# Four layers in one kernel: the first half's row maxima taken in fp32 before the operands are split

## The chip, the cores and the metric

The kernel runs on one core of one Trainium2 chip. The metric is the device time of one execution in microseconds. Engines: TensorE (PE; PEld for its weight loads), VectorE (DVE), ScalarE (ACT), GpSimd (POOL) and SyncE (SP), which here only issues DMAs. They run side by side and wait for each other by semaphores that the kernel sets by hand.

## What is computed

The input x is (4, 32, 32, 32): 4 images b, 32 channels, 32 x 32 pixels. Four layers follow, each on the normalised sum so far and added to it:

```python
x = x + volterra(norm(x))        # layer 0: 3x3 taps and their pairwise products
x = x + conv3x3(norm(x))         # layer 1
x = x + attention(norm(x))       # layer 2
x = x + hartley(norm(x))         # layer 3: transform, mix of modes, transform back
```

In layer 2 the image is projected (W_in); a 3x3 convolution gives q (all 1024 pixels), and two without padding give k and v (900 keys), in 4 heads of 8 channels. Per image and head: softmax over the keys of q.k, times v. The other three query and token pairs of the reference have a zero hidden state, so that of them only the mean of the value convolution over the image is left; it enters the gates as a bias (the "box sums"). Gates, a cell and an output projection end the layer.

## The kernel before

**Stages.** Layer 0 up to about 44 us, layer 1 to about 63, the projections of layer 2 to about 93, its attention to about 290, layer 3 to the end.

**Attention.** Queries are handled in 8 halves (2 halves of the pixels x 4 images), each with 4 heads and 4 tiles of 128 queries. exp(q.k - max) needs each query's maximum over 900 keys first. So each half has two passes on TensorE. The *maxima*: 16 rows of work (head, query tile), two blocks of 450 keys each (L1110, bf16). In the first two halves, and for 3 rows in 8 later, the pair is "diff" and "first": ScalarE takes the ReLU of q.(k2 - k1) (L646), VectorE adds it to q.k1 and takes the maximum (L841); otherwise VectorE reduces both blocks (L846). After a half's last block VectorE *splits* the 16 negated maxima into three bfloat16 parts (L818 to L825), TensorE *turns* them (L1116), VectorE copies them (L855) and GpSimd's queue sends them by DMA into three more rows of the query operand (L576, semaphore m_in). The *scores*: 28 tiles of 128 keys and one of the remaining 4 keys per head (L1133, L1138); ScalarE takes their exponentials (L638), TensorE multiplies by the turned values (L1151, L1156), in groups of four tiles. The first score of a half waits for its m_in.

**Operands.** fp32 accuracy comes from bf16 parts: q and k are each split into three bf16 parts by ScalarE and VectorE in turns (L611 to L625, L764 to L794), written to DRAM by SP (L479, L482), and read back stacked, 72 rows of 8 channels x 9 products (L490, L498). The maxima cannot start before the first stack is in.

**Order.** attention_plan() writes one list that all engines follow: maximum blocks, splits, turns, scores and value groups. It takes the first half's 32 blocks and its turn, FIRST_AHEAD = 18 more, then per step of four scores and one value group BLOCKS_PER_STEP = 4.15 more. A turn is moved MOVED = 4 blocks back. The first 44 blocks use six PSUM banks, later ones three (L411).

**Before the attention**, on TensorE: input projection (L1048, K = 128 rows, three column tiles), k convolution, window product, q convolution, box sums (L1078, 72 matmuls of one column), v convolution (all L1060), their products (L1085), turned values (L1091). Where TensorE has to wait, matmuls on zeros are meant to keep its clock: keep_clock (L960, 128 rows), keep_clock_rows (L969, 9 rows in each of four row groups), keep_clock_columns (L975).

## Time and profile before

| | us |
|---|---|
| median of 3 runs | 339.88 (339.66 to 342.13) |
| profiled execution, whole | 339.74 |
| its span, first to last instruction | 337.9 |
| TensorE busy in the span | 311.3 |
| VectorE busy | 208.7 |
| ScalarE busy | 178.0 |

Busy times are sums over stages with different limits, so they have to be read by stage. In the trace an fp32 matmul is two instructions, a matmul's length contains its run-out, and consecutive ones overlap: a count and the time of the whole group tell what one costs. The clock is TensorE's granted clock, 1.0 for 2.4 GHz.

### The profile page before, as it was taken

Reading aid. Unit: us, or ns where it says so; the run is one execution under the profiler, and the core shown is the slowest. Engines: PE = TensorE matmul, PEld = TensorE weight load, DVE = VectorE, ACT = ScalarE, POOL = GpSimd, SP = SyncE. Lnnn points to the kernel's source line nnn. Section 1 sums busy time; section 2 is a strip of 40 time slices with the busy share of each in tenths; the row PEclk is TensorE's granted clock in tenths of the full one; section 3 lists DMA queues with packets and bytes.
Section 4 is the critical chain, followed back from the end, with each engine's and each line's share of the span. In section 5 each row is a group of like instructions: output and inputs, shape, how many; then the busy total and the mean of one; then the engine's idle time right before and its main releaser. Section 6 shows DMA issues by size and latency. Waiting matters only on the chain.

```text
span 337.9 us, 7025 instructions
## 1 busy us (share of the span) xinstructions
PE 311.3 (92%) x2827; PEld 120.5 (36%) x2827; DVE 208.7 (62%) x472; ACT 178.0 (53%) x337; POOL 33.4 (10%) x35
## 2 busy tenths in 40 slices
PE   5999989999988999999999999999999899977793
PEld 1689523234322223323323223322232222423751
DVE  4970362577288337686868878867787221477364
ACT  1100101135185768787887969888788788300400
POOL 6910400000000000100101001010010100000000
PEclk9999978999896569999999999999999999997798
DMA  7000000005650854750000000000000000000001
GB/s 257 31 4 4 2 0 0 3 0 151 161 121 18 157 132 113 278 250 3 2 3 0 3 2 2 0 2 4 2 0 2 2 3 0 0 2 1 4 2 62
DMA packets 3756, 15.05 MB, mean 45 GB/s; under 512 B 804, under 2 KB 1572, under 8 KB 3308
## 3 DMA queue, kind: packets, MB, share of 16 engines
q1 hardware_dynamic: 3468, 14.50, 14.7%
q8 instruction: 22, 0.36, 0.4%
q0 software_dynamic: 256, 0.11, 0.2%
q14 instruction: 10, 0.08, 0.1%
HBM read 12.13 MB, written 2.37 MB: 43 GB/s over the span
## 4 chain that ended last, share of the span: by engine, by line
PE 79%; DVE 12%; issue 4%; ACT 3%; DMA 1%; ACTq 0%; DVEq 0%
PE ps L1151 16%; PE ps L1133 16%; PE ps L1110 15%; PE ps L998 9%; PE ps L1060 3%; PE ps L1254 3%; PE ps L960 2%; PE ps L1048 2%; ACT arena_b L638 2%; PE ps L1156 2%; PE ps L1209 2%; PE ps L1034 2%; PE ps L1026 1%; PE ps L969 1%; DVE arena_a L921 1%
## 5 line engine op out<-in xcount | busy, mean ns | idle before, releaser
L638 ACT ACTIVATE arena_b<-ps 128x512 f32<-128x512 f32 x232 | 125.4, 605 | 32.3 <-PE ps L1133 31.3
L1110 PE MATMUL ps<-arena_a 72*128 72x450 bf16 x256 | 89.3, 378 | 1.4 <-DVE vrest L811 0.8
L1133 PE MATMUL ps<-arena_a 75*128 75x512 bf16 x224 | 86.7, 397 | 0.7 <-ACT arena_b L638 0.3
L846 DVE TENSOR_REDUCE mx<-ps 128x1 f32<-128x450 f32 x120 | 69.3, 618 | 6.8 <-PE ps L1110 5.8
L841 DVE CUSTOM_DVE_ANT_0 sums<-ps,relus 128x450 bf16<-128x450 f32 x68 | 41.3, 626 | 35.7 <-PE ps L1110 29.7
L1151 PE MATMUL ps<-arena_b,vt 128*32 128x512 f32 x448 | 61.4, 621 | 0.7 <-ACT arena_b L638 0.7
L1133 PEld LDWEIGHTS ps<-arena_a 75*128 75x128 bf16 x224 | 21.9, 99 | 72.5 <-ACT arena_b L638 43.9
L646 ACT ACTIVATE relus<-ps 128x450 f32<-128x450 f32 x68 | 37.3, 552 | 7.0 <-PE ps L1110 7.0
L1110 PEld LDWEIGHTS ps<-arena_a 72*128 72x128 bf16 x256 | 24.2, 101 | 36.9 <-DVE mx L841 9.4
L960 PE MATMUL ps<-zeros 128*128 128x512 bf16 x76 | 21.2, 425 | 4.4 <-DMA xa<-x 3.9
L998 PE MATMUL ps<-arena_b,arena_a 32*32 32x512 f32 x720 | 24.6, 610 | 0.0
L998 PEld LDWEIGHTS ps<-arena_b,arena_a 32*32 32x32 f32 x720 | 21.2, 103 | 2.6
L1060 PE MATMUL ps<-arena_b,cst 128*32 128x450 f32 (+1 forms) x144 | 17.5, 616 | 0.0
L597 ACT ACTIVATE arena_b<-ps 128x512 f32<-128x512 f32 x2 | 1.1, 595 | 28.2 <-PE ps L998 28.2
L576 POOL DMA_DIRECT2D arena_a<-mt_sb x8 | 5.2, 646 | 105.0 <-DVE mt_sb L855 105.0
L1151 PEld LDWEIGHTS ps<-arena_b,vt 128*32 128x32 f32 x448 | 8.9, 109 | 18.5 <-ACT arena_b L638 13.4
L704 DVE SCALAR_TENSOR_TENSOR arena_b<-xp 128x1122 f32<-128x1122 f32 (+2 forms) x12 | 14.8, 1316 | 0.0
L960 PEld LDWEIGHTS ps<-zeros 128*128 128x128 bf16 x76 | 7.5, 106 | 17.0 <-issue 10.9
L665 ACT ACTIVATE arena_a<-arena_a,cst 128x1024 f32<-128x1024 f32 x4 | 4.3, 1138 | 17.1 <-DVE arena_a L921 17.1
L583 POOL TENSOR_TENSOR on<-ot,rden 128x512 f32<-128x512 f32 x7 | 7.3, 1038 | 58.7 <-DVE rden L865 58.7
L863 DVE STREAM_TRANSPOSE ot<-ps 128x512 f32<-128x512 f32 x8 | 5.7, 712 | 11.0 <-PE ps L1156 11.0
L1254 PE MATMUL ps<-arena_b,arena_a 128*64 128x64 f32 x256 | 9.2, 245 | 3.5 <-ACT arena_a L665 3.5
(135 smaller groups left out, 240.8 us busy)
## 6 DMA issues: line engine op xcount, KB each, us to landing
arena_b<-wmodes SPq DMA_DIRECT2D x1, 4096.0 KB, 13.3
arena_a<-k_scratch SPq DMA_DIRECT2D x9, 258.4 KB
arena_a<-q_scratch SPq DMA_DIRECT2D x12, 96.0 KB
arena_a<-q_scratch SPq DMA_DIRECT2D x3, 384.0 KB
k_scratch<-arena_b SPq DMA_DIRECT2D x3, 344.5 KB, 3.3
cst<-consts SPq DMA_DIRECT2D x1, 967.5 KB, 7.8
arena_a<-k_scratch SPq DMA_DIRECT2D x6, 129.2 KB
q_scratch<-arena_b SPq DMA_DIRECT2D x6, 128.0 KB, 4.8
```

What stands on the lines that cost most here:

```text
L638: nc.scalar.activation(probs[:, n % PRING, :], ps[:, SCORE_RING[n % len(SCORE_RING)], :], ACT.Exp).then_inc(expd, 1)
L646: nc.scalar.activation(relus[:, d % 3, :], ps[:, block_bank(i), 0:KHALF], ACT.Relu).then_inc(max_relu, 1)
L704: nc.vector.scalar_tensor_tensor(maps[:, 1 + m, 0:n], xp[:, 0:n], VOLTERRA_SCALE, xp[:, at:at + n], ALU.mult, ALU.mult).then_inc(map_ready, 1)
L841: nc.vector.tensor_tensor_reduce(out=sums[:, d % 2, :], in0=bank, in1=relus[:, d % 3, :], scale=1.0, scalar=-3.0e38, op0=ALU.add, op1=ALU.max,
L846: nc.vector.tensor_reduce(mx[:, a, e:e + 1], bank, AX.X, ALU.max).then_inc(max_read, 1)
L960: mm(ps[:, bank, :], zeros[:, 0:P], zeros[:, 0:512], start=True, stop=True)
L998: last = mm(ps[column, b, :].rearrange("p (y x) -> p y x", x=W // 2), l0w[row, 2 * r + i, :], window(image, py, px + 16 * e, 0, H, W // 2) ...
L1060: last = mm(ps[32 * b:32 * b + 32, bank + e, 0:ny * cols].rearrange("p (y x) -> p y x", x=cols), weights[:, px, :], window(xst[:, b, :], f ...
L1110: mm(ps[:, block_bank(i), 0:KHALF], qst[0:PAIR_ROWS, e, g, qt * P:(qt + 1) * P], kst[0:PAIR_ROWS, g, at:at + KHALF], start=True, stop=True ...
L1133: last = mm(ps[:, bank, :], kst[0:S_ROWS, g, t * P:(t + 1) * P], qst[0:S_ROWS, e, g, :], start=True, stop=True)
L1151: last = mm(ps[32 * h:32 * h + 32, bank, :], vt[:, t, half % B * HEADS + h, :], probs[:, (n0 + h) % PRING, :], start=(t == 0), stop=False, ...
L1254: last = mm(banks(4 * k2, 4)[64 * jh:64 * jh + 64, 64 * l:64 * l + 64], xv[:, k2, l, jh], wv[:, k2, l, jh], start=True, stop=True)
```

## The change

- The first half's maxima (half 0) are taken in fp32. Three matmuls with a constant "spread" matrix put each head's 8 channels of k1, k2 - k1 and q of image 0 at the head of a group of 32 rows, the rest zero (kf, qf). A block is then one fp32 matmul on one head's 32 rows (first_block). Its 32 blocks stand in one run, in pairs of heads: diff, diff, first, first; five PSUM banks in turn.
- Box sums (a2), value convolution (v), their products (gb), the second half of the q convolution (q1) and the turned values (vt) stand behind the 32 blocks; half 0's turn stands after the first of three parts of v's second half. VectorE's list has the same order: a2, gb, split, turn, vt.
- FIRST_AHEAD is 6, BLOCKS_PER_STEP 4.4. From half 1 on blocks are as before.
- ScalarE makes the high bf16 parts of k and q; GpSimd makes both low parts (low_parts, three operations for each of three ranges of k and for each half of q). SP stacks a whole image at a time.
- The input projection takes 32 x 32 tiles: four row groups (images) x three column tiles. The k convolution waits for the copies alone, no longer for GpSimd's padding.
- keep_clock_rows and keep_clock_columns go; 11 and 8 full zero matmuls stand in their places. The keep_clock ahead of the maxima goes.

```diff
-FIRST_AHEAD = 18
-WIDE_AHEAD = 12
-BLOCKS_PER_STEP = 4.15
+FIRST_RING = (0, 1, 2, 3, 4)
+FIRST_AHEAD = 6
+BLOCKS_PER_STEP = 4.4
...
-    for s in range(2 * B):
+    for qt in range(HALF_TILES):
+        for h in range(0, HEADS, 2):
+            for kind in ("diff", "first"):
+                for a in (h * HALF_TILES + qt, (h + 1) * HALF_TILES + qt):
+                    stream.append(("max", i, 0, a, kind))
+                    i += 1
+    stream.append(("split", 0))
+    stream.append(("turn", i, 0))
+    i += 1
+    for s in range(1, 2 * B):
...
-    for at in [at for at, item in enumerate(stream) if item[0] == "turn"]:
+    for at in [at for at, item in enumerate(stream) if item[0] == "turn" and item[2] > 0]:
...
-    take(2 * ROWS_OF_MAX + 1 + FIRST_AHEAD)
+    take(2 * ROWS_OF_MAX)
+    plan += [("a2",), ("v", 0, 0), ("v", 0, 1), ("v", 0, 2), ("gb",), ("v", 1, 0)]
+    take(1)
+    plan += [("v", 1, 1), ("v", 1, 2), ("vs",), ("q1",), ("vt",)]
+    take(FIRST_AHEAD)
...
-        prologue = 2 * ROWS_OF_MAX + WIDE_AHEAD
+        prologue = 2 * ROWS_OF_MAX
         def block_bank(i):
-            ring = SCORE_RING + MAX_RING if i < prologue else MAX_RING
+            ring = FIRST_RING if i < prologue else MAX_RING
...
+            high = (k_high, len(K_RANGES)), (q_high, 1)
+            rest = ((k_split, 3 * len(K_RANGES) - 1), (q_split, 2)), ((k_split, 3 * len(K_RANGES)), (q_split, 3))
+            for s, (k_wait, q_wait) in enumerate((high, *rest)):
+                sp.wait_ge(*k_wait)
                 sp.dma_start(k_dram[:, s].rearrange("c g n -> g c n"), k_parts[:, s, :]).then_inc(kd_written, 16)
-            for s in range(PARTS):
-                sp.wait_ge(q_part[s], 1)
+            for s, (k_wait, q_wait) in enumerate((high, *rest)):
+                sp.wait_ge(*q_wait)
                 sp.dma_start(q_dram[s, 0].rearrange("c g n -> g c n"), q_parts[:, s, 0:HALF]
                              ).then_inc(qd_written[0], 16)
...
-            stack_k(0, 0, HEADS // 2)
+            stack_k(0, 0, HEADS)
             sp.wait_ge(qd_written[0], PARTS * 16)
             stack_q(0, 0, 0, HEADS)
-            stack_k(1, HEADS // 2, HEADS)
-            stack_k(2, HEADS, 2 * HEADS)
+            stack_k(1, HEADS, 2 * HEADS)
             stack_q(1, 0, HEADS, 2 * HEADS)
             sp.wait_ge(m_in, 16)
-            stack_k(3, 2 * HEADS, 3 * HEADS)
-            stack_q(2, 0, 2 * HEADS, 3 * HEADS)
-            stack_k(4, 3 * HEADS, G)
-            stack_q(3, 0, 3 * HEADS, G)
-            for s in range(PARTS):
-                sp.wait_ge(q_part[s], 2)
+            for b in (2, 3):
+                stack_k(b, b * HEADS, (b + 1) * HEADS)
+                stack_q(b, 0, b * HEADS, (b + 1) * HEADS)
...
+            def low_parts(whole, res, parts, split, n):
+                nc.gpsimd.tensor_tensor(res, whole, parts(0), ALU.subtract).then_inc(split, 1)
+                pool.wait_ge(split, n + 1)
+                nc.gpsimd.tensor_copy(parts(1), res).then_inc(split, 1)
+                pool.wait_ge(split, n + 2)
+                nc.gpsimd.tensor_tensor(parts(2), res, parts(1), ALU.subtract).then_inc(split, 1)
+            for i, cols in enumerate(K_RANGES):
+                pool.wait_ge(k_high, i + 1)
+                low_parts(kc[:, cols], k_res[:, cols], lambda s: k_parts[:, s, cols], k_split, 3 * i)
+            def low_query(e):
+                half = slice(e * HALF, (e + 1) * HALF)
+                pool.wait_ge(q_high, e + 1)
+                pool.wait_ge(qc_act, e + 1)
+                low_parts(qc[:, half], qc[:, half], lambda s: q_parts[:, s, half], q_split, 3 * e)
+            pool.wait_ge(spread_done, 3)
+            low_query(0)
...
+                    low_query(1)
...
+            act.wait_ge(k_done, 1)
+            nc.scalar.activation(kc[:, 0:KHALF], ps[:, 2, 0:KHALF], ACT.Copy).then_inc(kc_act, 1)
+            nc.scalar.activation(k_parts[:, 0, 0:KHALF], ps[:, 2, 0:KHALF], ACT.Copy).then_inc(k_high, 1)
+            act.wait_ge(kc_zeroed, 1)
+            for i in (1, 2):
+                act.wait_ge(kc_dve, i)
+                nc.scalar.activation(k_parts[:, 0, K_RANGES[i]], kc[:, K_RANGES[i]], ACT.Copy).then_inc(k_high, 1)
+            def high_query(e, bank):
                 half = slice(e * HALF, (e + 1) * HALF)
                 act.wait_ge(q_done, e + 1)
-                nc.scalar.activation(q_parts[:, 0, half], ps[:, 4 + e, :], ACT.Copy).then_inc(q_part[0], 1)
-                act.wait_ge(dve_step, Q_RESID[e])
-                nc.scalar.activation(q_parts[:, 1, half], q_res[:, half], ACT.Copy).then_inc(q_part[1], 1)
-            act.wait_ge(v_done, 2)
-            nc.scalar.activation(vs.rearrange("p (a n) -> p a n", a=2), ps[:, 6:8, 0:KHALF],
-                                 ACT.Copy).then_inc(vs_ready, 1)
+                nc.scalar.activation(qc[:, half], ps[:, bank, :], ACT.Copy).then_inc(qc_act, 1)
+                nc.scalar.activation(q_parts[:, 0, half], ps[:, bank, :], ACT.Copy).then_inc(q_high, 1)
+            high_query(0, 4)
+            act.wait_ge(spread_done, 1)
+            nc.scalar.activation(kf[:, 0:KHALF], ps[:, 0, 0:KHALF], ACT.Copy).then_inc(first_act, 1)
+            act.wait_ge(spread_done, 3)
+            nc.scalar.activation(qf, ps[:, 2, :], ACT.Copy).then_inc(first_act, 1)
...
+            dve.wait_ge(k_done, 2)
+            nc.vector.tensor_copy(kc[:, KHALF:KEYS], ps[:, 3, 0:KHALF]).then_inc(kc_dve, 1)
+            dve.wait_ge(kc_act, 1)
+            nc.vector.tensor_tensor(kc[:, KDIFF:KW], ps[:, 3, 0:KHALF], kc[:, 0:KHALF], ALU.subtract).then_inc(kc_dve, 1)
+            dve.wait_ge(spread_done, 2)
+            nc.vector.tensor_copy(kf[:, KHALF:KEYS], ps[:, 1, 0:KHALF]).then_inc(first_dve, 1)
...
+                elif item[0] == "a2":
+                    dve.wait_ge(a2_done, 1)
+                    nc.vector.tensor_copy(a2[:], ps[:, 5, 0:1]).then_inc(a2_ready, 1)
+                elif item[0] == "gb":
+                    dve.wait_ge(gb_done, 1)
+                    link(nc.vector.tensor_tensor(gb[:], ps[:, 5, 8:11], c_("gbias"), ALU.add))
+                    for i in (0, 2):
+                        nc.vector.tensor_scalar(gb[:, i:i + 1], gb[:, i:i + 1], 0.5, None, ALU.mult).then_inc(gb_ready, 1)
+                elif item[0] == "vt":
+                    turn_values()
...
             pe.wait_ge(l0_read, 4)
-            keep_clock_rows(3)
+            keep_clock(6, 11)
...
-            keep_clock_columns(6, 1)
-            keep_clock_rows(1)
-            keep_clock_columns(6, 1)
+            keep_clock(6, 8)
...
+            win = c_("win")
+            for e in range(2):
                 for r in range(3):
-                    last = mm(ps[32 * r:32 * r + 32, (2 + n) % 8, :].rearrange("p (y x) -> p y x", x=W),
-                              c_("win")[:, 32 * b:32 * b + 32],
-                              window(xp, r, 1, 16 * e, 16, W), start=True, stop=True)
-                last.then_inc(xin_done, 1)
-            def conv(bank, weights, rows, cols, first, signal):
+                    for b in range(B):
+                        row = slice(32 * b, 32 * b + 32)
+                        n = e * B + b
+                        last = mm(ps[32 * r:32 * r + 32, (2 + n) % 8, :].rearrange("p (y x) -> p y x", x=W),
+                                  win[row, 32 * b:32 * b + 32], window(xp[row], r, 1, 16 * e, 16, W),
+                                  start=True, stop=True)
+                        if r == 2:
+                            last.then_inc(xin_done, 1)
...
+            for e in range(2):
+                pe.wait_ge(xin_act, 2 * (e + 1))
+                pe.wait_ge(xin_dve, 2 * (e + 1))
+                for px in range(3):
+                    last = conv(2 + e, qkv[:, 1], KH, KH, 1, e, px)
+                last.then_inc(k_done, 1)
             pe.wait_ge(win_ready, 6)
-            mm(ps[:, 0, 16:25], c_("win"), win9[:, 0, :], start=True, stop=True).then_inc(win_done, 1)
-            conv(4, qkv[:, 0], H, W, 0, q_done)
-            pe.wait_ge(win_scaled, 1)
...
+            mm(ps[:, 5, 16:25], c_("win"), win9[:, 0, :], start=True, stop=True).then_inc(win_done, 1)
+            pe.wait_ge(xin_ready, 1)
+            for px in range(3):
+                last = conv(4, qkv[:, 0], H, W, 0, 0, px)
+            last.then_inc(q_done, 1)
+            pe.wait_ge(kc_act, 1)
+            mm(ps[:, 0, 0:KHALF], c_("spread", 0, 32), kc[0:32, 0:KHALF], start=True, stop=True).then_inc(spread_done, 1)
+            pe.wait_ge(kc_dve, 2)
+            mm(ps[:, 1, 0:KHALF], c_("spread", 0, 32), kc[0:32, KDIFF:KW], start=True, stop=True).then_inc(spread_done, 1)
+            pe.wait_ge(qc_act, 1)
+            pe.wait_ge(k_high, 1)
+            mm(ps[:, 2, :], c_("spread", 0, 32), qc[0:32, 0:HALF], start=True, stop=True).then_inc(spread_done, 1)
...
+            def first_block(i, a, kind):
                 before = block_before(i, block_bank(i))
                 if before is not None:
+                    pe.wait_ge(*blocks_read[before])
+                h, qt = divmod(a, HALF_TILES)
+                row = slice(32 * h, 32 * h + 32)
+                at = {"first": 0, "diff": KHALF}[kind]
+                mm(ps[:, block_bank(i), 0:KHALF], qf[row, qt * P:(qt + 1) * P], kf[row, at:at + KHALF],
+                   start=True, stop=True).then_inc(max_scored, 1)
...
-            pe.wait_ge(q_part[2], 2)
-            keep_clock(2, 3)
-            pe.wait_ge(k_in[0], PARTS * 16)
-            pe.wait_ge(q_in[0], PARTS * 16)
-            pe.wait_ge(vt_ready, 2 + HEADS)
...
+                if item[0] == "v":
+                    _, e, px = item
+                    if e == 1 and px == 0:
+                        pe.wait_ge(xin_ready, 2)
+                    last = conv(6 + e, qkv[:, 2], KH, KH, 1, e, px)
+                    if px == 2:
+                        last.then_inc(v_done, 1)
+                elif item[0] == "a2":
+                    value_sums()
+                elif item[0] == "gb":
+                    gate_biases()
+                elif item[0] == "q1":
+                    pe.wait_ge(gb_ready, 2)
+                    for px in range(3):
+                        last = conv(5, qkv[:, 0], H, W, 0, 1, px)
+                    last.then_inc(q_done, 1)
+                elif item[0] == "vt":
+                    turn_values()
+                elif item[0] == "max" and item[2] == 0:
+                    if item[1] == 0:
+                        pe.wait_ge(q_high, 1)
+                        pe.wait_ge(first_act, 2)
+                        pe.wait_ge(first_dve, 1)
+                    first_block(item[1], item[3], item[4])
```

Not shown: names and semaphores, the new places in SBUF and PSUM, value_sums, gate_biases and turn_values, which hold the matmuls that stood in line before, and VectorE's identity copy and memset, which move ahead.

## Rows read from the trace of the kernel before

**Rows 1.** The page's first two parts: TensorE's busy time, its clock in 40 slices.
```profile
PE 311.3 (92%) x2827; PEld 120.5 (36%) x2827; DVE 208.7 (62%) x472; ACT 178.0 (53%) x337; POOL 33.4 (10%) x35
...
PEclk9999978999896569999999999999999999997798
```
**Rows 2.** Stretches: busy time by engine (PE, PEld, DVE, ACT, POOL), clock, DMA.
```profile
48.00:53.00 5.00, 5.00 (x21) 1.40 (x19) 0.37 (x2) 1.47 (x3) 0.00 (x0) 0.51 0.00 0
...
83.00:89.60 6.60, 6.60 (x57) 1.95 (x55) 1.24 (x3) 0.63 (x1) 0.00 (x0) 0.74 0.58 175
...
93.50:104.70 11.20, 9.54 (x37) 2.46 (x37) 9.89 (x38) 9.60 (x18) 0.61 (x5) 0.97 0.40 86
...
110.30:118.30 8.00, 8.00 (x25) 2.24 (x25) 3.17 (x10) 6.15 (x12) 0.00 (x0) 0.50 0.84 164
...
139.20:160.70 21.50, 21.50 (x124) 6.71 (x123) 17.23 (x41) 17.74 (x37) 1.68 (x2) 1.00 0.42 177
```
**Rows 3.** Groups by line: busy us, mean ns of one | idle before, releasers.
```profile
L638 ACT ACTIVATE arena_b<-ps 128x512 f32<-128x512 f32 x232 | 125.4, 605 | 32.3 <-PE ps L1133 31.3
...
L841 DVE CUSTOM_DVE_ANT_0 sums<-ps,relus 128x450 bf16<-128x450 f32 x68 | 41.3, 626 | 35.7 <-PE ps L1110 29.7 <-ACT relus L646 5.0 <-issue 0.6
L646 ACT ACTIVATE relus<-ps 128x450 f32<-128x450 f32 x68 | 37.3, 552 | 7.0 <-PE ps L1110 7.0
...
L583 POOL TENSOR_TENSOR on<-ot,rden 128x512 f32<-128x512 f32 x7 | 7.3, 1038 | 58.7 <-DVE rden L865 58.7
...
L755 DVE TENSOR_REDUCE wsum<-xp 128x32 f32<-128x960 f32 x3 | 3.2, 1129 | 0.0
...
L747 DVE TENSOR_SCALAR arena_b<-ps,cst 96x512 f32<-96x512 f32 x4 | 3.0, 747 | 5.0 <-PE ps L1048 5.0
```
**Rows 4.** Timeline, TensorE, 44 to 70 us: start, us, engine, line, operation, count.
```profile
44.23 3.70 PE L969 MATMUL ps<-zeros 9*128 9x512 f32 x24 [1.23 <-DVE xb L718]
...
53.04 5.32 PE L1034 MATMUL ps<-arena_b,l1s 96*128 96x512 f32 x12
...
60.27 1.14 PE L969 MATMUL ps<-zeros 9*128 9x512 f32 x8
...
62.88 6.66 PE L1048 MATMUL ps<-xp,cst 128*32 128x512 f32 x45 [0.47 <-DVE xp L689]
```
**Rows 5.** Timeline, TensorE, 75 to 95 us: convolutions, box sums, first blocks.
```profile
75.72 5.36 PE L1060 MATMUL ps<-arena_b,cst 128*32 128x512 f32 x48
...
81.00 2.13 PE L1078 MATMUL ps<-win,cst 32*32 32x1 f32 x72
...
83.07 6.50 PE L1060 MATMUL ps<-arena_b,cst 128*32 128x450 f32 x48
...
93.52 1.49 PE L1110 MATMUL ps<-arena_a 72*128 72x450 bf16 x7 [0.77 <-DVE vrest L811]
```
**Rows 6.** Timeline, 103 to 111 us: split, turn and first score.
```profile
103.49 0.19 DVE L818 TENSOR_REDUCE negm<-mx 128x16 f32<-128x32 f32 x1
...
104.66 0.27 PE L1116 MATMUL ps<-ident_b,mparts 128*48 128x128 bf16 x1 [1.33 <-DVE mparts L825]
...
110.62 0.63 PE L1133 MATMUL ps<-arena_a 75*128 75x512 bf16 x1
```
**Rows 7.** Timeline, 240 to 245 us: a late half's turn, its DMA, its first score.
```profile
240.71 0.24 PE L1116 MATMUL ps<-ident_b,mparts 128*48 128x128 bf16 x1
...
241.77 0.63 POOL L576 DMA_DIRECT2D arena_a<-mt_sb  x1 [13.08 <-DVE mt_sb L855]
...
243.99 1.06 PE L1151 MATMUL ps<-arena_b,vt 128*32 128x512 f32 x8
...
244.98 0.39 PE L1133 MATMUL ps<-arena_a 75*128 75x512 bf16 x1
```
**Rows 8.** DMA issues: count, KB each, median us to landing.
```profile
q_scratch<-arena_b SPq DMA_DIRECT2D x6, 128.0 KB, 4.8
...
arena_a<-mt_sb POOLq DMA_DIRECT2D x8, 12.0 KB, 2.2
```

300 lines of the change are left out of this document (133 added, 167 removed).

## The prediction

> **What bounds the kernel now.** I read the page's engine shares and clock line first, then busy times in stretches, then groups by line, then the timeline where an engine waits. The page gives TensorE 92% of the span, and a clock line with dips [rows 1]. The stretches say where that counts. In the half from 139.2 to 160.7 us TensorE is busy 21.50 of 21.50 us at full clock, ScalarE 17.74, VectorE 17.23 [rows 2]: from there until the maximum blocks run out a microsecond of TensorE is a microsecond of the kernel. Ahead of it lies a chain through all engines: first maximum block at 93.52 us [rows 5], first score at 110.62 us [rows 6].
>
> The clock is the second thing to see. It is at 1.2 GHz (about 0.5) in 48 to 53 us, in part of 83 to 89.6, and in 110.3 to 118.3 [rows 2]. Ahead of the first dip stand zero matmuls of 9 rows [rows 4]; ahead of the second, 72 matmuls of one column [rows 5]; ahead of the third, the run of maxima and the split. In 110.3 to 118.3 TensorE is busy 8.00 of 8.00 us, on 72 to 75 rows, and stays at 0.50 [rows 2]. So being busy is not enough: light matmuls lose the clock, and do not bring it back.
>
> **The change, in order of time.**
>
> *Clock-keeping.* Full-array zero matmuls replace the 9-row ones. The 5.00 us of work in 48 to 53 us at 0.51 [rows 2] would take half. I take 2.5 us off; bounds 0 (it falls anyway) and 2.5. The normalised image is then there at 60.4 instead of 62.88 us [rows 4].
>
> *Input projection.* Today 45 of its 48 instructions take 6.66 us on three tiles [rows 4]; on twelve tiles that is about a quarter, 1.8 us (bounds: 1.7 if all overlap; 2.3 if no better than eight instructions in 1.14 us on four row tiles, against 0.443 each in a plain queue, 5.32 us for 12 [rows 4]). What then sets the pace is the copies: VectorE's four take 3.0 us [rows 3], 61.4 to 64.4. The key convolution no longer waits for GpSimd's padding; its half begins at 63.0 and the whole (48 instructions, about 5.3 us as [rows 5]) ends at 68.3.
>
> *Up to the first block.* VectorE's window sums (3.2 us [rows 3] and some 0.6 for the small reduces) end at 68.2; their product on TensorE, about 0.5, delays the query convolution to 68.8. Only its first half now stands here: half of 5.36 us [rows 5], to 71.5. Three spreading matmuls on one row group, six fp32 instructions at 0.39 to 0.44 us by the plain-queue row [rows 4], end at 73.95; ScalarE's copy of the query, 0.6 [rows 3] plus 0.2 to start, makes it 74.8. The blocks start 18.7 us earlier than 93.52 [rows 5]; the trip of the operands through DRAM has left this path.
>
> *The 32 blocks.* A block was one bf16 instruction, seven in 1.49 us [rows 5]; it is now two fp32 instructions on 32 rows, 0.78 us at 2.4 GHz. Different row groups overlap [rows 4], so PSUM banks and readers set the pace. A bank is held for the block (0.78), a start-up of 0.2, its reader (ScalarE 37.3 us for 68, 0.55 each; VectorE 0.63 [rows 3]) and 0.13 to hand it back; two blocks of a kind end together, so the second waits 0.55, 0.27 on average: about 1.9 us over five banks, 0.38 a block, 12.2 us for 32. At 1.2 GHz the block is 1.56 and the bank time 2.7: 0.54 a block, 17.3 us, with fill about 18.
>
> Which clock? Ahead of the run TensorE does 2.45 us of matmuls on 32 of 128 rows, stands 0.8 us, and then keeps some two of four row groups at work. The nearest rows are the 9-row tiles, with the fall inside their 3.70 us [rows 4], and the busy stretch that stays at 0.50 [rows 2]. I take 1.2 GHz from about the start of the blocks, not given back during them: blocks issued to 92.8 us. The other end is the full clock: 87.0.
>
> A rule speaks for that other end. The Trainium skill, "TensorE: Matmul & The Clock Gate", section "Why this matters for your kernels", has mid-kernel drops come from idle gaps between bursts of matmuls. There is no long gap here, so by it the clock holds and the first rival below is the result. This trace does not bear it out: 8.00 of 8.00 us busy at 0.50.
>
> *Behind the blocks*, at the low clock: box sums 2.1 [rows 5], to 95; half the value convolution, 2.7 doubled less its narrower rows, 4.5, to 99.5; the products of the sums 0.6. On VectorE the split is queued behind the gate biases, which wait for these products: it idles from 94, does the biases (0.5) and the split (103.49 to the turn at 104.66 [rows 6], 1.2), and TensorE's turn, with all that stands behind it, comes at 101.8. Then two parts of the value convolution (3.0 low), the second query half (2.7 to 5.3; the clock comes back within a convolution, as in 83 to 89.6 [rows 2], so 3.5), the turned values 1.4, six blocks 1.8: first score at 111.5, against 110.62 [rows 6]: +0.9; the turn's DMA, 3.3 us (below), is in by 105.2. With the full clock the same items are 2.1, 2.6, 0.6, 1.7, 1.8, 2.7, 1.4 and 2.1: 102.1 us; with the dip behind the box sums that today stretches 48 convolution instructions from 5.36 to 6.50 [rows 5], 103.2.
>
> *GpSimd's low parts.* Twelve operations of 450 to 512 columns, near the 1.04 us of its one tensor-tensor row [rows 3]: 67 to some 80 us, on GpSimd ahead of the first turn's DMA (101.8). SP writes q after that (landing 4.8 [rows 8]) and stacks from about 85. They are needed by the second half's first blocks, at 110 (100 with the full clock): nothing, the cover being the run of maxima. At twice the price they end at 92 and the stacks near 105: still nothing at the low clock, up to 5 us at the full one.
>
> *Fewer blocks ahead of the scores*, 6 instead of 18. Twelve move into the stretch where TensorE is the bound: 12 x 0.2 [rows 5] = +2.4. All blocks of the second half are ScalarE pairs; in three more steps four exponentials (125.4 us for 232, 0.54 each [rows 3]) and 2.2 ReLUs (0.5) take 3.25 us against TensorE's 2.75, less what today has of that: +1.0.
>
> *The turn comes late.* Count the stream. Half k's turn is number 37 + 33k. Before, 51 + 31.5k are taken when half k's first score comes: 14 - 1.5k blocks of lead. After, 39 + 33.4k: a lead of 2 + 0.4k. Today's closest is k = 6: turn at 240.71, its DMA issued at 241.77, 2.2 to land [rows 7, 8], so 3.3 us, and the score at 244.98 [rows 7] finds it there. After, between turn and score stand at k = 1 two blocks and one values group (0.17 + 0.4 + 1.06 [rows 7], 1.65 us); at k = 2 also the remainder score (2.0); at k = 3 and 4 one more block (2.2); at 5 and 6 two values groups (3.6, enough). TensorE, and every block, value group and score behind that first score, waits 1.65 + 1.3 + 1.1 + 1.1 = 5.2 us. Bounds 0 (if something else holds TensorE there) and 6.5.
>
> *Sum.* +0.9 + 2.4 + 1.0 + 5.2 = +9.5 on the profiled execution's 339.74 (span 337.9 and 1.84 around it; 0.14 under the median 339.88): **349 us**.
>
> **Rivals.** (A) *The clock holds through spreads and blocks.* The blocks keep two row groups busy, more than today's 72 rows at part time (9.54 of 11.20 us at 0.97 [rows 2]); against it, the spreads. First score 103.2: -7.4 + 2.4 + 1.0 + 5.2 = +1.2: 341 us.
>
> (B) *Faster: no dip anywhere up to the end of the first half.* Place: from the spreads to the first value groups. Today the first scores run at 0.50 [rows 2], two steps at some 5.2 us instead of 3.25. Held, first score 102.1 (-8.5), those two steps -4: -8.5 - 4 + 2.4 + 1.0 + 5.2 = -3.9: 336 us; should the turn's wait vanish too, 331. It decides from where the six blocks and the first scores, light again, keep the clock; today the same light mix does not.
>
> (C) *Row tiles do not overlap in issue order.* Then 32 x 0.78 = 25 us, 13 more than in A: 354, or far above at the low clock. [rows 4] speaks against it.
>
> **How the numbers follow.** Forecast 0.48 (own range 344 to 353: fill, when the clock returns, 0 to 6.5 of the turn's wait); A 0.22; B 0.20; C 0.10. A measurement of this kernel tells some 1% from no change. Faster by over 1%: B and a little of A, 0.22. Within 1%: the rest of A and the lowest of the forecast, 0.24. Slower: 0.54. The range reaches to B's 334 and to 353; above it lies C, below it a B without the turn's wait.
>
> **What would show it.** Right: first block near 75 us; the clock at 0.5 in most of the blocks, which then take 17 to 19 us; split some 6 us after the last maximum was read; first score near 111; idle TensorE of 1 to 2 us ahead of the first scores of halves 1 to 4, put down to the maxima's DMA. Wrong: a clock of 1.0 through the blocks (A or B); halves 1 to 4 as busy as today's 21.50 of 21.50; a first block waiting for k or q (GpSimd's price).

## The result, and the profile after

| | kernel before | changed kernel |
|---|---|---|
| time, median of four (range) | 339.81 us (339.66 to 342.13) | 348.69 us (346.69 to 353.64) |
| ratio, 95% interval | | 1.0225 [1.0136, 1.0314] |
| profiled execution (span) | 339.74 us (337.94) | 353.64 us (351.51) |

The change makes the kernel slower, by 1.4 to 3.1%. The changed kernel's profiled execution is the longest of its four (the others took 346.69, 347.13 and 350.24 us): the ratio leaves it out, and its trace holds more lost clock than theirs.

The page of the changed kernel: engine shares, TensorE's busy tenths and the granted clock in 40 slices (beside [rows 1]):

```profile
PE 316.6 (90%) x2833; PEld 128.7 (37%) x2833; DVE 204.3 (58%) x466; ACT 176.6 (50%) x338; POOL 46.6 (13%) x49
...
PE   4999887999998999898998999999999799896694
...
PEclk9999999975569579999999999999999699998998
```

The dip of before at 48 to 53 us has gone. There is a longer one in slices 9 to 12, a second in 14 to 15 and a third in slice 32 (a slice is 8.8 us).

TensorE's timeline of the changed kernel, from the input projection to the first score (start, duration, instructions, idle time before and its releaser; beside [rows 4 to 6]):

```profile
60.47 2.21 PE L1064 MATMUL ps<-xp,cst 32*32 32x512 f32 x48 [1.70 <-DVE xp L737]
63.38 4.90 PE L1074 MATMUL ps<-arena_b,cst 128*32 128x450 f32 x48 [0.69 <-DVE arena_b L796]
...
68.69 2.78 PE L1074 MATMUL ps<-arena_b,cst 128*32 128x512 f32 x24
71.41 1.02 PE L1096 MATMUL ps<-arena_b,cst 32*128 32x450 f32 x2
...
73.02 1.02 PE L1101 MATMUL ps<-arena_b,cst 32*128 32x512 f32 x2
74.77 19.43 PE L1139 MATMUL ps<-arena_a 32*128 32x450 f32 x64 [0.73 <-ACT arena_a L670]
94.13 3.44 PE L1108 MATMUL ps<-win,cst 32*32 32x1 f32 x72
97.50 4.73 PE L1074 MATMUL ps<-arena_b,cst 128*32 128x450 f32 x24
102.16 0.80 PE L1116 MATMUL ps<-a,cst 32*32 32x1 f32 x24
102.88 0.98 PE L1074 MATMUL ps<-arena_b,cst 128*32 128x450 f32 x8
104.48 0.22 PE L1159 MATMUL ps<-ident_b,mparts 128*48 128x128 bf16 x1 [0.61 <-DVE mparts L844]
104.62 4.33 PE L1074 MATMUL ps<-arena_b,cst 128*32 128x450 f32 x40
...
112.30 0.55 PE L1153 MATMUL ps<-arena_a 72*128 72x450 bf16 x2 [0.80 <-DVE mx L861]
112.69 0.38 PE L1179 MATMUL ps<-arena_a 75*128 75x512 bf16 x1
```

The first block (L1139) starts 18.75 us earlier than in [rows 5], the first score (L1179) 2.07 us later than in [rows 6]. All that was gained ahead of the blocks is spent between the two.

Busy times and granted clock of the changed kernel by stretch (columns as in [rows 2]):

```profile
44.00:75.00 31.00, 25.95 (x185) 9.74 (x188) 18.89 (x48) 8.06 (x15) 7.54 (x11) 1.00 0.05 12
75.00:105.00 30.00, 29.39 (x197) 17.69 (x198) 11.09 (x42) 8.03 (x16) 4.21 (x5) 0.54 0.48 110
105.00:112.70 7.70, 6.64 (x62) 2.41 (x54) 2.93 (x9) 3.00 (x6) 1.53 (x7) 1.00 0.45 105
112.70:126.40 13.70, 13.70 (x43) 3.64 (x42) 4.04 (x15) 9.72 (x19) 2.85 (x3) 0.51 0.59 131
```

In 75 to 105 us TensorE is busy 29.39 of 30.00 us at 0.54, that is at 1.2 GHz for nearly all of it. The clock comes back at about 102.7 and is lost again behind the first score. The second dip is not in every execution. Experiments 8 and 10 below give TensorE the same matmuls in the same order up to there; in their traces the clock comes back at 99.0 and 99.5 us and holds through the first scores, and the first half's scores take 20.8 us from first to last where they take 25.8 here. The stretch in the trace of experiment 10:

```profile
105.00:131.00 26.00, 24.19 (x146) 7.23 (x139) 13.25 (x44) 22.42 (x47) 3.59 (x8) 1.00 0.56 135
```

The second half's turn: the DMA of its maxima (GpSimd's queue), the half's first score, and the wait over the whole execution (us in total, times, longest):

```profile
139.65 0.62 POOL L618 DMA_DIRECT2D arena_a<-mt_sb  x1 [23.96 <-DVE mt_sb L885]
```
```profile
141.88 0.39 PE L1179 MATMUL ps<-arena_a 75*128 75x512 bf16 x1 [1.24 <-DMA arena_a<-mt_sb]
```
```profile
PE ps L1179 <- DMA arena_a<-mt_sb: 4.2, 4, 1.2
```

Before, the nearest such score found its maxima there [rows 7]. Now four halves wait, 1.24, 1.18, 1.11 and 0.68 us.

The last turn, which no step of the prediction named:

```profile
273.94 0.27 PE L1159 MATMUL ps<-ident_b,mparts 128*48 128x128 bf16 x1 [1.90 <-DVE mparts L844]
274.15 1.94 PE L1197 MATMUL ps<-arena_b,vt 128*32 128x512 f32 x8
...
281.01 1.07 PE L1197 MATMUL ps<-arena_b,vt 128*32 128x512 f32 x8 [0.36 <-ACT arena_b L680]
```

Eight value matmuls take 1.94 us behind it and 1.07 us seven microseconds later: the clock fell in that wait.

**The difference, added up** between the profiled executions, by the starts of the remainder scores (L1138 before, L1184 after), the last scores of a half: +2.07 us at the first score; +0.71 to the end of the first half's scores (25.08 to 25.79); +9.07 over the next five halves (107.20 to 116.27), of which 4.21 are the four waits and 4.86 something else; +3.51 over the last two (42.85 to 46.36), where the clock fell at the last turn; -1.79 from there to the end (52.19 to 50.40), mostly layer 3, which the change leaves as it was. The sum is +13.57, the difference of the spans.

### The profile page after: what moved, and what is told of

Same layout as the page of the kernel before. It is cut to its first block, busy times and chain, and to the rows that moved or that the text cites. A ratio compares the mean times of both kernels' runs of the same rounds, so it can differ in the third digit from the quotient of the medians.

```text
span 351.5 us, 7042 instructions
## 1 busy us (share of the span) xinstructions
PE 316.6 (90%) x2833; PEld 128.7 (37%) x2833; DVE 204.3 (58%) x466; ACT 176.6 (50%) x338; POOL 46.6 (13%) x49
## 4 chain that ended last, share of the span: by engine, by line
PE 62%; DVE 17%; issue 12%; DMA 4%; ACT 4%; POOL 1%; ACTq 0%; DVEq 0%; SPq 0%; POOLq 0%
PE ps L1197 11%; PE ps L1179 10%; PE ps L1153 9%; PE ps L1013 8%; PE ps L1139 6%; PE ps L1074 3%; DMA arena_a<-mt_sb 2%; PE ps L1311 2%; ACT arena_b L680 2%; DVE mx L866 2%; DVE sums L861 2%; PE ps L1266 2%; PE ps L1202 2%; PE ps L1049 1%; DMA xa<-x 1%
## 5 line engine op out<-in xcount | busy, mean ns | idle before, releaser
L1179 PE MATMUL ps<-arena_a 75*128 75x512 bf16 x224 | 87.2, 400 | 4.9 <-DMA arena_a<-mt_sb 4.2
L1153 PE MATMUL ps<-arena_a 72*128 72x450 bf16 x224 | 78.6, 369 | 2.4 <-DVE mx L861 1.7
L1197 PE MATMUL ps<-arena_b,vt 128*32 128x512 f32 x448 | 63.1, 637 | 0.7 <-ACT arena_b L680 0.7
L1179 PEld LDWEIGHTS ps<-arena_a 75*128 75x128 bf16 x224 | 22.0, 100 | 78.1 <-ACT arena_b L680 43.8
L1153 PEld LDWEIGHTS ps<-arena_a 72*128 72x128 bf16 x224 | 22.0, 100 | 34.2 <-DVE mx L866 9.3
L990 PE MATMUL ps<-zeros 128*128 128x512 bf16 x92 | 23.8, 404 | 6.3 <-DMA xa<-x 4.0
L1139 PE MATMUL ps<-arena_a 32*128 32x450 f32 x64 | 19.4, 972 | 0.7 <-ACT arena_a L670 0.7
L990 PEld LDWEIGHTS ps<-zeros 128*128 128x128 bf16 x92 | 8.8, 103 | 20.3 <-issue 9.6
L1139 PEld LDWEIGHTS ps<-arena_a 32*128 32x128 f32 x64 | 12.5, 297 | 7.1 <-issue 4.8
```

Source lines behind the costliest of these rows:

```text
L990: mm(ps[:, bank, :], zeros[:, 0:P], zeros[:], start=True, stop=True)
L1139: mm(ps[:, block_bank(i), 0:KHALF], qf[row, qt * P:(qt + 1) * P], kf[row, at:at + KHALF], start=True, stop=True).then_inc(max_scored, 1)
L1153: mm(ps[:, block_bank(i), 0:KHALF], qst[0:PAIR_ROWS, e, g, qt * P:(qt + 1) * P], kst[0:PAIR_ROWS, g, at:at + KHALF], start=True, stop=True ...
L1179: last = mm(ps[:, bank, :], kst[0:S_ROWS, g, t * P:(t + 1) * P], qst[0:S_ROWS, e, g, :], start=True, stop=True)
L1197: last = mm(ps[32 * h:32 * h + 32, bank, :], vt[:, t, half % B * HEADS + h, :], probs[:, (n0 + h) % PRING, :], start=(t == 0), stop=False, ...
```

## The experiments

**1. The early part alone.** In the kernel before:

```
-            keep_clock_rows(3)
+            keep_clock(6, 11)
...
-            keep_clock_columns(6, 1)
-            keep_clock_rows(1)
-            keep_clock_columns(6, 1)
+            keep_clock(6, 8)
...
-            for n in range(2 * B):
-                e, b = divmod(n, B)
-                for r in range(3):
+            win = c_("win")
+            for e in range(2):
+                for r in range(3):
+                    for b in range(B):
+                        row = slice(32 * b, 32 * b + 32)
...
-                              c_("win")[:, 32 * b:32 * b + 32],
-                              window(xp, r, 1, 16 * e, 16, W), start=True, stop=True)
+                                  win[row, 32 * b:32 * b + 32], window(xp[row], r, 1, 16 * e, 16, W),
+                                  start=True, stop=True)
```

> The kernel before with the early part of the change alone: full-array zero matmuls (11 and 8) instead of the 9-row ones, and the input projection on twelve 32 x 32 tiles. My theory: the early part is a gain that the rest of the change spends again. The normalised image 2.5 us earlier (60.4) and some 5 us less up to the end of the projection's copies, so the first maximum block at 87 to 89 instead of 93.52 us and about 334 us in all; the part of the change behind the spreads then costs some 13 us. Rival: everything ahead of the first block also waits for transfers through DRAM or for VectorE, so the gain is swallowed and the time stays at 338 to 341; the rest of the change then costs 7 to 8 us.

Measured: 332.50 us (329.95 to 333.46), ratio 0.9763 [0.9711, 0.9815]. The first block is at 85.20, 8.3 us earlier than in [rows 5], the first score at 104.37:

```profile
85.20 1.49 PE L1112 MATMUL ps<-arena_a 72*128 72x450 bf16 x7 [0.77 <-DVE vrest L811]
...
104.37 0.63 PE L1135 MATMUL ps<-arena_a 75*128 75x512 bf16 x1
```

So the early part is worth 7.3 us by the medians, and the rest of the change costs 16.2, the difference to 348.69.

**2. Zero matmuls at the spreads and among the blocks.**

```
             mm(ps[:, 0, 0:KHALF], c_("spread", 0, 32), kc[0:32, 0:KHALF], start=True, stop=True).then_inc(spread_done, 1)
+            keep_clock(6, 2)
...
+            keep_clock(6, 2)
...
+            keep_clock(6, 4)
...
                     first_block(item[1], item[3], item[4])
+                    if item[1] % 2:
+                        keep_clock(6, 1)
```

> The changed kernel with full-array zero matmuls into an unused bank: two, two and four behind the three spreading matmuls, and one behind every second block of the run of 32. Nothing else is changed. My theory (the clock is lost to light matmuls, and the low clock costs 8.3 us up to the first score): the granted clock stays at 1.0 through the blocks, they take 12 to 13 us instead of 19.4, the first score comes at 104 to 106 instead of 112.7, and the time falls by 6 to 8 us, to 340 or so. Rival 1: the blocks are paced by the banks and their readers whatever the clock: the clock is kept and the run still takes 17 to 19 us, 346 to 349. Rival 2: the clock falls in spite of the zero matmuls, which then add 24 x 0.43 us on TensorE: 350 or more.

Measured: 351.73 us (346.52 to 351.99). The clock is 1.00 in 75 to 96.5 us, and the run of blocks takes 20.4 us all the same:

```profile
76.06 1.02 PE L1142 MATMUL ps<-arena_a 32*128 32x450 f32 x4
77.02 0.39 PE L990 MATMUL ps<-zeros 128*128 128x512 bf16 x1
77.34 1.02 PE L1142 MATMUL ps<-arena_a 32*128 32x450 f32 x4
```

The time is rival 2's, but not by its reason: the clock is kept, and the run is longer than even rival 1's 17 to 19 us. In the rows a pair of blocks (0.96 us) no longer runs beside the next, since a zero matmul on all rows stands between. The run did not price the clock; experiment 5 does.

**3. Eighteen blocks ahead.**

```
-FIRST_AHEAD = 6
+FIRST_AHEAD = 18
```

> The changed kernel with 18 instead of 6 blocks of the second half ahead of the first score (as many as before the change). My theory: no half's first score waits for its turn any more (between turn and score there are then 14 or more blocks and four value groups, over 9 us, against 3.3 us for the turn's DMA), 4.2 us less; the 12 blocks cost some 0.4 us each ahead of the first score (4 to 5 us, at the low clock and paced by their readers) and save 2.4 us later: 343 to 347 in all. Rival (something else holds TensorE at the starts of the halves): the idle time there goes to another releaser and the time stays at 347 to 350.

Measured: 348.84 us (347.20 to 351.44). No first score waits for its maxima any more. But the first score comes at 118.48, 5.8 us later than in the changed kernel, and the halves without a wait still take 22.1 to 22.9 us against 21.4 before. My theory of the waits held and its time did not: the gain was spent ahead of the first score and in the halves. Experiment 12 shows by what.

**4. More blocks to a step.**

```
-BLOCKS_PER_STEP = 4.4
+BLOCKS_PER_STEP = 4.8
```

> The changed kernel with 4.8 instead of 4.4 blocks to a step of four scores, and still six blocks ahead. Between turn and first score there are then 3.6, 4.8, 7.3 and 9.7 us of TensorE's work at halves 1 to 4 instead of 1.5, 1.7, 1.9 and 1.9. My theory: the waits of 1.24, 1.18, 1.11 and 0.68 us for the maxima's DMA vanish, and since the blocks are the same and only come earlier, the time falls by up to 4 us, to 343 to 345. Rival: a step with 4.8 blocks is bound by ScalarE or VectorE, which read them; the idle time of TensorE comes back as waits for their readers, and the time stays within 1% of 347.

Measured: 360.89 us (352.05 to 365.85). Both expectations missed it. The waits are gone, but from 168 to 264 us a half takes 23.5 to 24.4 us (VectorE is busy 18.9 us of 24, and 16.7 of 21.4 before), and the last turn now waits 3.02 us, behind which the clock was low from 273 to 287 us. A step with more blocks costs more than TensorE's 0.2 us for each.

**5. Zero matmuls at the spreads only**, the first three additions of experiment 2 without the last.

> The changed kernel with eight full-array zero matmuls (2, 2 and 4) behind the three spreading matmuls and none among the blocks. The run before kept the clock but laid a zero matmul between every two pairs of blocks: a pair then took 1.28 us (0.96 and 0.32) and the 32 blocks 20.4 us, so it did not show the price of the clock by itself. My theory: the clock is lost ahead of the blocks, by the spreads and the wait for the query's copy; kept there, it holds, and with nothing between the pairs the blocks take 12 to 14 us from 76.1; first score at 104 to 106, the whole 341 to 344. Rival 1: what paces the blocks is the pair (two row groups at work, then the next two on the same rows, 0.96 us): 15 to 16 us at full clock, first score at 107 to 108, about 344 to 346. Rival 2: the blocks are too light themselves, the clock falls within the first third of the run, and the whole is where it was or 1.3 us above.

Measured: 344.96 us (342.32 to 346.39), ratio 1.0137 [1.0073, 1.0201].

```profile
75.72 12.87 PE L1142 MATMUL ps<-arena_a 32*128 32x450 f32 x64
88.53 2.13 PE L1111 MATMUL ps<-win,cst 32*32 32x1 f32 x72
...
103.39 0.38 PE L1182 MATMUL ps<-arena_a 75*128 75x512 bf16 x1
```
```profile
105.00:116.00 11.00, 11.00 (x37) 2.62 (x36) 3.32 (x11) 7.80 (x16) 1.32 (x2) 0.53 0.62 141
```

My theory holds in the rows, and its time (341 to 344) is missed by 1 us: at full clock the blocks take 12.87 us, and the first score is 9.3 us earlier. The gain by the medians is only 3.7 us. In this trace the clock falls at the first scores, and the first half's scores end at 127.92; in the traces of experiments 8 and 10, which lost it in the blocks but not there, they end at 130.48 and 131.48.

**6. The early part, and a zero matmul behind every block.** To experiment 1:

```
                     max_block(*item[1:])
+                    if not started:
+                        keep_clock(7, 1)
...
+                    started = True
                     score_tile(item[1])
+                    if item[1] < 8:
+                        keep_clock(7, 1)
```

> The kernel before with the early part of the change (332.5 us in the first experiment, with the clock at 0.5 from 89.7 to 113.6 us), and one full-array zero matmul into an unused bank behind every maximum block up to the first score and behind each of the first eight scores. The blocks here are one bfloat16 pass on 72 rows, so nothing runs beside them that a zero matmul could hold up, and they are paced by their readers (0.34 us each in the run). My theory: the clock stays at 1.0 over the whole stretch; the first score comes at about 103 instead of 104.4, the first half's scores end 6 us earlier, at 121 instead of 127.3, and the time is 325 to 328. Rival: the zero matmuls (some 58 of 0.21 us, 12 us) lie on the path at full clock and eat what the clock gives: 331 to 335.

Measured: 329.67 us (329.46 to 330.97), ratio 0.9709 [0.9654, 0.9764]. The clock is at 1.0 up to 304 us, but the first score comes at 106.49 and the first half's scores end at 126.75, 0.5 us earlier than without. Between theory and rival: the zero matmuls eat most of what the clock gives.

**7. Zero matmuls at the first scores.** In the changed kernel:

```
+                    if item[1] == 0:
+                        pe.wait_ge(vt_ready, 2 + HEADS)
                     score_tile(item[1])
+                    if item[1] < 8:
+                        keep_clock(7, 1)
```

(The wait lets VectorE read the turned values out of that bank first.)

> The changed kernel with one full-array zero matmul behind each of the first eight scores. In the changed kernel the clock is at 0.5 from 113.0 to 126.7 us, and the half's last score comes 25.8 us after its first; where the clock was kept up to there (second experiment) it was 20.8 us. My theory: the clock stays at 1.0 behind 112.7, the first half gets 3.5 to 5 us shorter, and the time is 342 to 345. Rival: the first steps are paced by the readers of the blocks and by the exponentials, whatever the clock; the half stays at 24 us or more and the time within 1% of 347.

Measured: 351.90 us (349.97 to 355.09), ratio 1.0359 [1.0286, 1.0433]. Two stretches, and the first score of the second half:

```profile
111.00:138.00 27.00, 24.48 (x136) 7.83 (x137) 13.40 (x44) 22.04 (x46) 3.83 (x7) 1.00 0.50 119
138.00:146.00 8.00, 8.00 (x25) 2.35 (x24) 4.07 (x9) 4.86 (x10) 1.04 (x1) 0.57 0.97 395
```
```profile
137.00 0.39 PE L1179 MATMUL ps<-arena_a 75*128 75x512 bf16 x1 [2.09 <-DMA arena_a<-mt_sb]
```

The first half takes 21.2 us from first to last score, 4.6 less than in the changed kernel's trace. But experiments 8 and 10 take 20.8 without a zero matmul there, so this is a gain only over an execution that lost the clock at this place. Behind it the wait at the next half is 2.09 us instead of 1.24, the clock falls there, and that half takes 27.86 us instead of 23.86. Both expected times are missed.

**8. The split first.** The list takes the split straight behind the 32 blocks:

```
     take(2 * ROWS_OF_MAX)
+    plan.append(stream.pop(0))
```

> The changed kernel with the split of the first half's maxima ahead of the box sums' product and the gate biases on VectorE; the turn stays where it is on TensorE. My theory: the split is done at 96 instead of 104.3, the turn's wait of 0.61 us on TensorE goes, and nothing else moves, since the turn's DMA was in 5 us before the first score anyway: 0.6 us, within what one look can not tell from none. Rival: the early split brings the turn forward by the whole wait of VectorE (8 us), and the first score with it.

Measured: 348.96 us, one execution. The split is done at 94.8, the turn waits for nothing, and the first score is at 109.71 instead of 112.69. My theory of the 0.6 us holds in the rows; of the rest, 0.8 us stand ahead of the first block already (74.01), and the clock, which here came back at 99.0, is the other difference. Experiment 10 has the split in its old place and the clock back at 99.5: from the first block to the first score it takes 36.37 us, and this kernel 35.70, which is 0.67 less.

**9. Zero matmuls at every place**: experiments 5 and 7 together with

```
                 if i == 0:
+                    if 1 <= half <= 4:
+                        if half >= 2:
+                            pe.wait_ge(o_read, half - 1)
+                        keep_clock(O_RING[half % 2], 6)
                     pe.wait_ge(m_in, 16 * (half + 1))
...
                 pe.wait_ge(*blocks_read[block_before(i, block_bank(i))])
+                if s == 2 * B - 1:
+                    keep_clock(block_bank(i), 8)
                 pe.wait_ge(m_split, s + 1)
```

> The changed kernel with full-array zero matmuls wherever a run so far lost the clock up to the end of the maxima: eight behind the spreads, one behind each of the first eight scores, six ahead of the first scores of halves 1 to 4 (they stand in the wait for the maxima's DMA, into the bank of the values that is free then), and eight in the wait of the last turn. This is the case of my second rival in full (no dip anywhere). My theory: where the clock was kept in one place only, the next light stretch lost it, so the gains did not add up; kept everywhere, first score at 103 to 104, first half's scores done by 125 (127.9 where it fell at the first scores), no low clock between 75 and 300 us, and 336 to 339 in all, still above 332.5 of the early part alone, since the waits at halves 1 to 4 (some 5 us) and the slower halves stay. Rival: the zero matmuls at the waits lengthen them and the time stays at 343 to 346.

Measured: 346.95 us (341.50 to 347.28).

```profile
75.00:89.00 14.00, 14.00 (x78) 7.95 (x77) 8.86 (x31) 8.48 (x17) 3.79 (x4) 1.00 0.72 172
89.00:97.00 8.00, 8.00 (x121) 4.26 (x122) 0.86 (x6) 0.00 (x0) 0.00 (x0) 0.57 0.52 113
106.00:118.00 12.00, 11.79 (x36) 3.85 (x37) 3.39 (x13) 7.04 (x13) 3.21 (x6) 0.57 0.70 154
118.00:300.00 182.00, 177.56 (x996) 54.08 (x997) 118.15 (x283) 139.52 (x274) 11.70 (x14) 1.00 0.09 31
```

The expectation fell: the clock now goes in the box sums (one column each), the one light stretch left without zero matmuls, and again at the first scores. The execution that lost least (mean clock 0.986) took 341.5 us, above the kernel before.

**10. Zero matmuls in the last turn's wait alone**, the second addition of experiment 9.

> The changed kernel with eight full-array zero matmuls in the last turn's wait alone, into the bank that the turn writes behind them. My theory: the last turn waits 1.90 us for VectorE's split (1.30 in the kernel before), and in most executions this loses the clock for 3.4 to 13.7 us (after the change, and in the second, fourth, seventh and eighth experiment; never in the four traces with a wait of 1.3 us): filled, no low clock between 265 and 290 us, and the slow end of the runs (350 to 354 us) goes: all runs at 344 to 349, median 346 to 347. Rival: the dip there follows the clock's history and not this wait; it is there again, and the runs spread from 346 to 354 as before.

Measured: 346.58 us (345.31 to 347.40), ratio 1.0186 [1.0107, 1.0266].

```profile
264.80 1.89 PE L990 MATMUL ps<-zeros 128*128 128x512 bf16 x8
266.78 0.24 PE L1161 MATMUL ps<-ident_b,mparts 128*48 128x128 bf16 x1
266.95 1.06 PE L1199 MATMUL ps<-arena_b,vt 128*32 128x512 f32 x8
```

As expected, the value matmuls behind the turn take 1.06 us, no dip stands in 264 to 290 us (clock 1.00), and none of the four executions took over 347.40 us. The last two halves take 43.85 us instead of 46.36, so the filled wait is worth 2.5 us in the traces. That it removed the long executions is not shown: the span is 7.6 us shorter than the changed kernel's, and 7.0 of it stand ahead of the first half's last scores (131.48 against 138.48), where the two kernels are the same. Some 7 us over the kernel before remain.

**11. Half as many zero matmuls.** To experiment 6:

```
-                    if not started:
+                    if not started and item[1] % 2:
```

> The sixth experiment (early part alone, 329.7 us) with a zero matmul behind every second maximum block instead of every one ahead of the first score. There the 32 blocks and the rest of the run were paced by block and zero matmul together (0.41 us) and the first score came at 106.5, behind the 104.4 of the kernel without them. My theory: half as many keep the clock too and lie beside the readers (0.34 us a block): first score at 102.5 to 104, 326.5 to 328 in all. Rival: with half as many the clock falls in the run, the first half is as without them, and the time is 331 to 333.

Measured: 327.23 us (325.02 to 344.00), ratio 0.9593 [0.9515, 0.9671]. Three of the four executions took 325.0 to 327.7 us, and the ratio is theirs; the fourth took 344.00 at a mean clock of 0.931, where the profiled one has 0.991, so this kernel can lose the clock as well. In the profiled one, the first score at 101.80, the first half's scores done at 122.18 (127.28 in experiment 1):

```profile
84.00:102.00 18.00, 15.86 (x78) 7.16 (x78) 15.82 (x58) 13.51 (x25) 1.43 (x6) 1.00 0.40 80
102.00:123.00 21.00, 20.80 (x119) 6.74 (x117) 12.05 (x36) 18.98 (x40) 0.60 (x1) 1.00 0.60 136
```

By its median this is the fastest version of all, below both kernels. The four executions of experiment 6, with twice the zero matmuls up to the first score, took 329.46 to 330.97 us.

**12. The planner's numbers of before.**

```
-FIRST_AHEAD = 6
-BLOCKS_PER_STEP = 4.4
+FIRST_AHEAD = 18
+BLOCKS_PER_STEP = 4.15
```

> The changed kernel with the planner's two numbers of before: 18 blocks ahead of the first score and 4.15 to a step, everything else as changed. Between two remainder scores (the last scores of a half) the kernel before takes 21.4 to 21.5 us, the changed one 22.8 to 23.9, of which 0.7 to 1.2 is the wait for the turn; with 18 ahead and 4.4 to a step (third experiment) the waits were gone and it was 22.1 to 22.9. My theory: what is left, 0.7 to 1.4 us a half, is the price of 1.9 more blocks in it, some 0.5 us each instead of the 0.2 of my sum, because a step with more blocks is held up by their readers now and then; with 4.15 the halves are 21.4 to 21.6 us again, and the time is 343 to 346. Rival: the halves are slower for another reason (the banks' new order, the operands' new places): they stay at 22 us or more and the time at 347 to 350.

Measured: 344.27 us (343.90 to 346.00), ratio 1.0102 [1.0058, 1.0146]. Remainder scores of two neighbouring halves, first of this kernel, then of the changed one:

```profile
162.83 0.40 PE L1184 MATMUL ps<-arena_a 75*32 75x512 bf16 x4
184.30 0.40 PE L1184 MATMUL ps<-arena_a 75*32 75x512 bf16 x4
```
```profile
162.34 0.40 PE L1184 MATMUL ps<-arena_a 75*32 75x512 bf16 x4
185.58 0.40 PE L1184 MATMUL ps<-arena_a 75*32 75x512 bf16 x4
```

A half is 21.47 us, as before the change (157.21 to 178.68, 21.47), against 23.24. So all that the halves lost came from the planner's two numbers, and nothing from the new banks or places. What is left of the cost, 1.0% by the ratio and 5.8 us between the two traces' spans, lies ahead of the first half's last scores, at 141.32 (135.70 before).

Two more comparisons follow from this run. Experiment 3 has the same 18 blocks ahead and differs in the blocks to a step alone, 4.4 instead of 4.15. First and last remainder scores, of experiment 3 and of this one:

```profile
143.85 0.40 PE L1184 MATMUL ps<-arena_a 75*32 75x512 bf16 x4
298.57 0.40 PE L1184 MATMUL ps<-arena_a 75*32 75x512 bf16 x4
```
```profile
141.32 0.40 PE L1184 MATMUL ps<-arena_a 75*32 75x512 bf16 x4
291.36 0.40 PE L1184 MATMUL ps<-arena_a 75*32 75x512 bf16 x4
```

The seven halves take 154.72 and 150.04 us: 4.7 us for the same blocks taken faster. And against experiment 1, which has the same two numbers and the early part alone, this kernel is 11.8 us slower by the medians; the first half's last scores come 14.0 us later (141.32 against 127.28). That is what the fp32 maxima and the work moved behind them cost. How it divides between the blocks, the new order and the low clock was not measured apart.

## Why the prediction was right, point by point

**The number** came out better than its terms. The sum stands on a traced execution, and the changed kernel's traced execution is 13.57 us longer, not 9.5: the first score misses by +1.2, the first half and the denser steps by +2.2, the waits by -1.0, and the last turn (+3.5) and the end (-1.8) are not in the sum. The other executions lost less clock, and that their median with it lies 0.3 us from 349 is in part luck. The direction, the low clock in the blocks, the waits and their places were argued from the rows and came.

**Up to the first block** every step held: image 60.47 (60.4 said), projection 2.21 us (1.8 said, within its bounds), copies done at 64.55 (64.4), first block at 74.77 (74.8).

**The clock in the blocks**: lost from about the first of them (at 75.4 us) and not given back during them; 19.43 us against 18. The rival case, the clock kept, was run as experiment 5: 12.87 us against 12.2 said, and a first score at 103.39 against 103.2. The rule that spoke for it (the Trainium skill, "TensorE: Matmul & The Clock Gate", "Why this matters for your kernels") has the clock drop in idle gaps. Here it stays at 0.51 with TensorE busy 27.50 of 27.50 us (75.00 to 102.50), which the rule doesn't cover; at the last turn, where 1.90 us of waiting lost it in this trace, the rule's direction is borne out. What loses the clock ahead of the blocks stays open. The fall comes behind the three spreads and a wait of 0.73 us, and zero matmuls behind the spreads fill both; with them the same blocks keep 1.00 through 12.80 busy us (75.70 to 88.50 in experiment 5). So "light matmuls lose the clock" does not hold for these blocks by themselves. It does in experiment 1: there the clock fell at 89.7 us, amid bfloat16 blocks without a gap (87.0 to 95.5 us).

**Behind the blocks** three terms missed and nearly cancelled. The box sums took 3.44 us, not 2.1: I had taken a row measured at full clock, and 72 one-column matmuls do slow down with it (2.13 at full clock, experiment 5). The convolutions and turned values behind the turn took 5.5 us, not 7.9, since the clock came back ahead of the turn and not behind it. The six blocks took 2.56 us, not 1.8: their readers stand on VectorE behind six copies of the turned values that end at 111.57. First score at 112.69 against 111.5.

**The late split** began 8.4 us after the last maximum was read, not some 6, and cost TensorE 0.61 us (0.67 between experiments 8 and 10). That the turn comes late hurts nothing here, since its DMA has until the first score.

**GpSimd's low parts**: 67.10 to 79.4 us against 67 to 80, and no block waited for them, also where the blocks of the second half came at 100.8 (experiment 5).

**The turn's waits**: in the four halves named, put down to the DMA named; 4.2 us against 5.2. With a longer lead they vanish (experiments 3, 4 and 12).

**Fewer blocks ahead** is where the sum was wrong in kind. It has 12 x 0.2 = 2.4 us for twelve blocks moved behind the first score, and beyond +1.0 in the first half's steps nothing for taking the blocks at 4.4 instead of 4.15 to a step. The halves lost 4.86 us beside the waits, and experiments 3 and 12, which have the same blocks there, differ by 5.4 over the same five halves (4.7 over all seven). So the loss comes from the denser steps and not from the twelve blocks. A half is 21.4 us at 4.15, 22.1 to 22.9 at 4.4 without waits, 23.5 to 24.4 at 4.8: by these rows a block more in a half costs about half a microsecond, not TensorE's 0.2. VectorE and ScalarE read the blocks, and a step that holds more of them may be held up in pieces too short to show as waits; that these readers are the cause is argued from their busy times and was not shown apart.

**Not foreseen**: the clock lost at the last turn. It costs 2.5 of the 3.51 us over the last two halves, by the trace of experiment 10, where the wait is filled.

**Rival B** (faster, no dip anywhere) was wrong in its sum. Its place was right: with the clock at 1.00 at the first scores the first half takes 20.8 to 21.2 us (experiments 2, 7, 8 and 10), 4.6 to 5.0 less than in the profiled execution (4 said). But the waits at the next halves and the slower steps take it back, and no dip anywhere was not reached: 341.5 us was the best execution of experiment 9, against 336.

**What the sum hid**: that 349 is a gain of 7.3 us in the early part and a loss of 16 behind it. I had booked the earlier first block as one item and never asked what the projection alone would bring. Of the 16, the planner's two numbers are 4.4 by the medians (experiment 12) and the rest 11.8.

## What to carry to other kernels

Price the parts of a change that have no need of one another apart: here two of them were 7 us faster and the rest 16 us slower. Work packed more densely into a loop that several engines share can cost more than the engine that bounds the loop needs for it; here the same blocks at 4.4 instead of 4.15 to a step cost 4.7 us. Read a change that moves the clock from several executions, since one trace can hold a dip that the others have not. And where a stretch is light for TensorE, put a full-array zero matmul beside work that is paced by readers, not between matmuls that run side by side, and look at the next light stretch as well: a clock kept in one place only was lost in the next.

## What the runs showed that I had not expected

- A full-array matmul between row-tiled ones costs more than itself: 32 fp32 blocks on 32 rows take 12.87 us at full clock, 0.80 a pair; with a zero matmul behind each pair (some 0.24 us by itself, eight in 1.89 in experiment 10) a pair takes 1.28. The Trainium skill ("TensorE: Matmul & The Clock Gate", "Why this matters for your kernels") has tiles on different row groups run at the same time, and the 0.80 agrees.
- The clock goes with the last turn's wait: low behind it in five of the six traces in which TensorE waited 1.9 us or more there (the changed kernel, experiments 2, 4, 7 and 8; not 5), in none of the six with 1.27 to 1.30 us (before, experiments 1, 3, 6, 11 and 12), and in neither of the two in which zero matmuls fill it. The length alone does not decide: 1.91 us lost nothing in experiment 5, and 1.33 us ahead of the first turn [rows 6] lost it in the kernel before (1.00 up to 104.0 us, 0.50 from 104.25).
- The same instructions lose the clock for different times. The changed kernel and experiments 8 and 10 issue the same matmuls up to the first score; the clock came back at 102.7, 99.0 and 99.5 us, and fell again at the first scores in the first alone. Experiments 5 and 9 issue the same ones too up to the first score; the clock fell in the box sums in the second alone. So a dip in a single trace says what can happen and not what always does. Which of its dips made the 350.24 us execution longer than the other two is open, as only one execution has a trace.
